# A fused Flamingo block on one Trainium2 core: probabilities transposed once per pair of batches, value products on halves of the array, one bank for key and value projections

## What is computed

```python
q = (query @ wq).reshape(bs, sq, N_Q_HEADS, D_K).transpose((0, 2, 1, 3))
k = (key @ wk) ...
v = (value @ wv) ...
q = _apply_rope(q, curr_seq_pos)
k = _apply_rope(k, curr_seq_pos)
raw = jnp.einsum('bhqd,bhkd->bhqk', q, k) / scale
masked = raw + mask[:bs, None, curr_seq_pos:curr_seq_pos + sq, :sk]
attn = jax.nn.softmax(masked, axis=-1)
out = jnp.einsum('bhqk,bhkd->bhqd', attn, v)
out = out.transpose((0, 2, 1, 3)).reshape(bs, sq, N_Q_HEADS * D_V)
return out @ wo
```

## Time and profile before

| | us |
|---|---|
| median of 3 runs | 894.86 (893.86 to 894.96) |
| span of the profiled execution | 893.8 |
| first `score` to last `outputs` matmuls of the attention stage, in that execution | about 237 to 811 |
| PE busy, share of the span | 792.5, 89% |
| DVE busy, share of the span | 723.5, 81% |

### The profile page before, as it was taken

The page is one execution under the profiler, slowest core; times in us unless marked ns, Lnnn a source line. Parts: engine busy times, 40 slices in busy tenths (PEclk is TensorE's granted clock), DMA queues, the critical chain, the costliest instruction groups (busy, mean ns, idle before and its releaser), DMA issues. The chain is left out here.

```text
span 893.8 us, 13394 instructions
## 1 busy us (share of the span) xinstructions
PE 792.5 (89%) x4276; PEld 644.9 (72%) x4276; DVE 723.5 (81%) x1282; ACT 382.5 (43%) x1095; POOL 363.9 (41%) x300
## 2 busy tenths in 40 slices
PE   2899987977899999999999989999999999984764
PEld 1555653966688888778888878888887888873653
DVE  5898987879788888768888868888885988886994
ACT  2777774322343433434343334443433443243552
POOL 2777876233542532314433313353332432203562
PEclk9999999987999999999999999999999999997896
DMA  8210120110110211101021000111100102002001
GB/s 266 77 47 23 48 76 1 36 41 7 48 48 24 60 43 29 36 14 48 24 59 48 24 26 25 48 36 47 48 25 13 48 12 54 0 1 72 12 36 47
DMA packets 37443, 37.46 MB, mean 42 GB/s; under 512 B 2896, under 2 KB 27216, under 8 KB 37392
## 3 DMA queue, kind: packets, MB, share of 16 engines
q1 hardware_dynamic: 35168, 32.81, 12.7%
q10 hardware_dynamic: 2224, 3.94, 1.4%
HBM read 34.64 MB, written 2.10 MB: 41 GB/s over the span
## 5 line engine op out<-in xcount | busy, mean ns | idle before, releaser
L917 POOL TENSOR_TENSOR dense<-rope_a,rope_b 128x512 f32<-128x512 f32 x62 | 79.4, 1280 | 236.9 <-DVE rope_b L1037 236.9
L971 ACT ACTIVATE ot_hi<-PB 128x512 fp32r<-128x512 f32 x64 | 38.3, 598 | 182.7 <-PE PB L1286 182.7
L962 ACT ACTIVATE e_sb<-masked,nmax 128x64 f32<-128x64 f32 x256 | 86.1, 337 | 70.3 <-DVE nmax L1068 70.3
L1202 PE MATMUL QB<-xT_hi,wq_lo 128*128 128x512 f32 x256 | 107.9, 421 | 1.7 <-DVE xT_lo L1113 1.7
L1202 PE MATMUL ROW<-wo_hi,ot_lo 128*128 128x512 f32 x256 | 103.5, 404 | 5.7 <-DVE ot_lo L1087 5.7
L1204 PE MATMUL QB<-xT_hi,wq_hi 128*128 128x512 f32 x256 | 101.9, 398 | 2.1 <-issue 2.1
L1203 PE MATMUL QB<-xT_lo,wq_hi 128*128 128x512 f32 x256 | 102.1, 399 | 0.0
L1203 PE MATMUL ROW<-wo_lo,ot_hi 128*128 128x512 f32 x256 | 101.9, 398 | 0.0
L1204 PE MATMUL ROW<-wo_hi,ot_hi 128*128 128x512 f32 x256 | 101.8, 398 | 0.0
L1077 DVE TENSOR_TENSOR p_dup<-e_sb,rz 128x512 f32<-128x512 f32 x64 | 98.8, 1543 | 2.2
L1037 DVE TENSOR_TENSOR rope_b<-QB,rope 64x512 f32<-64x512 f32 x124 | 85.3, 688 | 3.9
(11 more groups left out here) (200 smaller groups left out, 2014.8 us busy)
## 6 DMA issues: line engine op xcount, KB each, us to landing
raw<-in_wq SPq DMA_DIRECT2D x32, 256.0 KB, 2.8
raw<-in_wo SPq DMA_DIRECT2D x32, 256.0 KB, 2.6
ctx_two<-in_ctx SPq DMA_DIRECT2D x16, 256.0 KB, 3.8
x_sb<-in_x SPq DMA_DIRECT2D x8, 256.0 KB, 7.9
ctx_raw<-in_ctxT ACTq DMA_DIRECT2D x1, 2048.0 KB, 13.4
raw<-in_wv SPq DMA_DIRECT2D x8, 256.0 KB, 2.8
raw<-in_wk SPq DMA_DIRECT2D x8, 256.0 KB, 2.9
out<-x_sb SPq DMA_DIRECT2D x8, 256.0 KB, 2.0
```

The lines of the kernel that those rows point to most:

```text
L917: nc.gpsimd.tensor_tensor(dst, a, b, ALU.add).then_inc(s_rot, 1)
L962: nc.scalar.activation(e_sb[:, r, :], masked[:, r, :], ACT.Exp, bias=nmax[:, r:r + 1], accum_out=zsum[:, r:r + 1]).then_inc(s_exp, 1)
L1202: nc.tensor.matmul(out, lhs[1], rhs[0], start=first, stop=False)
```

## The change

**Probabilities.** They are written once (`p_sb`, 128×256, in two alternating buffers) and ordered so that two batches of the same pair of heads stand side by side; 2 transposes of 128×128 then give, in the lower 64 rows, the first batch's and in the upper 64 rows the second batch's probabilities. pt_hi and pt_lo have 256 columns instead of 512, and normalizing waits for the transposes of two slots back instead of the last.

**Value products.** `v_stk` becomes `v_hi` and `v_lo`, each 128×256 per tile, rounded and split by one instruction each instead of two of 64 rows. `weighted` is 6 matmuls of 256 columns over 64 rows: v_lo·pt_hi, v_hi·pt_lo and v_hi·pt_hi, each for the lower and for the upper half of the array's rows. The halves write to two different banks (PB2).

**Projections.** Keys and values share one bank, KV, and so a key waits until the value ahead of it has been read out, and the other way round (`kv_free`). Values move to slots 0, 2, 3 (tiles 5 to 7 of the pair) and 10, 11, 12, 14, 15 (tiles 0 to 4 of the next); none is left in the slots with a key or after slot 15, and tile 4 of the first pair is made ahead of the first slot.

```diff
+V_OWN = {0: 5, 2: 6, 3: 7}
+V_NEXT = {10: 0, 11: 1, 12: 2, 14: 3, 15: 4}
...
-        v_stk = sb("v_stk", [P, B, 2 * DH], F32R)
+        v_hi = sb("v_hi", [P, TILES, 2 * DH], F32R)
+        v_lo = sb("v_lo", [P, TILES, 2 * DH], F32R)
...
-        KB, VB, SB_, TB, PB = (bank(n) for n in ("KB", "VB2", "SB", "TB", "PB"))
+        KV, SB_, TB = (bank(n) for n in ("KV", "SB", "TB"))
+        PB2 = ctx.enter_context(nc.psum_tensor("PB", [P, 2, 512], F32))
+        PB = [PB2[:, b, 0:256] for b in range(2)]
...
-                for b in range(2):
-                    rows = slice(S * b, S * b + S)
-                    nc.scalar.activation(v_stk[rows, 2 * tile + b, :], bank[rows, 0:2 * DH], ACT.Copy)\
-                      .then_inc(s_vhi, 1)
+                nc.scalar.activation(v_hi[:, tile, :], bank[:, 0:2 * DH], ACT.Copy).then_inc(s_vhi, 1)
...
-                if n:
-                    dve.wait_ge(s_t, N)
-                nc.vector.tensor_tensor(p_dup[:, :, :, :], e_sb[:, :, :].unsqueeze(2).broadcast_to([P, 4, 2, S]),
-                                        rz[:, :].unsqueeze(2).unsqueeze(3).broadcast_to([P, 4, 2, S]),
-                                        ALU.mult).then_inc(s_p, 1)
+                if n >= 2:
+                    dve.wait_ge(s_t, N - 1)
+                nc.vector.tensor_tensor(p_sb[:, n % 2, :, :], e_sb[:, :, :],
+                                        rz[:, :].unsqueeze(2).broadcast_to([P, 4, S]), ALU.mult).then_inc(s_p, 1)
...
-                for r in range(4):
+                for r in range(2):
                     mm = nc.tensor.transpose(TB[:, r * P:(r + 1) * P],
-                                             p_dup[:, r, :, :].rearrange("p a k -> p (a k)"), ident[:, :])
+                                             p_sb[:, n % 2, 2 * r:2 * r + 2, :].rearrange("p b k -> p (b k)"),
+                                             ident[:, :])
...
-                for b in range(2):
-                    v = v_stk[:, 2 * tile + b, g * DH:g * DH + DH]
-                    cols = slice(256 * b, 256 * b + 256)
-                    nc.tensor.matmul(PB[:, cols], v, pt_lo[:, cols], start=True, stop=False)
-                    mm = nc.tensor.matmul(PB[:, cols], v, pt_hi[:, cols], start=False, stop=True)
+                for i, (v, p) in enumerate(((v_lo, pt_hi), (v_hi, pt_lo), (v_hi, pt_hi))):
+                    for b in range(2):
+                        rows = slice(S * b, S * b + S)
+                        mm = nc.tensor.matmul(PB[b], v[rows, tile, g * DH:g * DH + DH], p[rows, :],
+                                              start=(i == 0), stop=(i == 2))
...
+            def kv_free(gp, n):
+
+                if n in (2, 10, 14):
+                    pe.wait_ge(s_parts, 3 * (q_job(gp, n - 1) + 1) + 3)
+                elif n == 9:
+                    pe.wait_ge(s_parts, 3 * (q_job(gp, 5) + 1) + 3)
+                elif n in V_OWN or n in (1, 5):
+                    pe.wait_ge(s_vlo, 8 * gp + 5 + sum(m < n for m in V_OWN))
+                else:
+                    pe.wait_ge(s_vlo, 8 * gp + 8 + sum(m < n for m in V_NEXT))
```

More of the change, by code:

```diff
@@ L834, in grouped_attention @@
         e_sb = sb("e_sb", [P, 4, S])
-        p_dup = sb("p_dup", [P, 4, 2, S])
+        p_sb = sb("p_sb", [P, 2, 4, S])
         nmax = sb("nmax2", [P, 4])
@@ L838, in grouped_attention @@
         rz = sb("rz2", [P, 4])
-        pt_hi = sb("pt_hi", [P, 512], F32R)
-        pt_lo = sb("pt_lo", [P, 512], F32R)
+        pt_hi = sb("pt_hi", [P, 256], F32R)
+        pt_lo = sb("pt_lo", [P, 256], F32R)
         ot_hi = sb("ot_hi", [P, GH, P], F32R)
@@ L859, in grouped_attention @@
         TX = [SB_, TB, QB[1], OB, SB_, TB, OB, SB_]
-        FIRST_V = [VB, PB, VB, PB]
+        FIRST_V = [PB2[:, t % 2, :] for t in range(5)]
         parts = (rope_a[:, :], rope_b[:, :])
-        spare_parts = (k_rot[:, 512:1024], p_dup[:, :, :, :].rearrange("p r a k -> p (r a k)"))
+        spare_parts = (k_rot[:, 512:1024], p_sb[:, :, :, :].rearrange("p n r k -> p (n r k)"))
         views = weight_views(d)
@@ L966, in round_pt @@
                 act.wait_ge(s_t, N + 1)
-                nc.scalar.activation(pt_hi[:, :], TB[:, :], ACT.Copy).then_inc(s_pthi, 1)
+                nc.scalar.activation(pt_hi[:, :], TB[:, 0:256], ACT.Copy).then_inc(s_pthi, 1)
             def round_ot(N):
@@ L986, in round_x @@
                                      ACT.Copy).then_inc(s_xhi, 1)
-            for tile in range(4):
+            for tile in range(5):
                 round_v(0, tile, FIRST_V[tile])
@@ L1002, in pair @@
                         round_ot(N - 1)
-                    if n < 4:
-                        round_v(gp, 4 + n)
-                    if 12 <= n < 15 and ahead:
-                        round_v(gp + 1, n - 12)
+                    if n in V_OWN:
+                        round_v(gp, V_OWN[n])
+                    if n in V_NEXT and ahead:
+                        round_v(gp + 1, V_NEXT[n])
                     for r, (kind, m, slot) in enumerate(OWN):
@@ L1016, in pair @@
                 round_ot(SLOTS * gp + SLOTS - 1)
-                if ahead:
-                    round_v(gp + 1, 3)
             with act.Fori(0, PAIRS - 1) as gp:
@@ L1132, in _ @@
                 normalize_x(t)
-            rest_v(0, 3, FIRST_V[3])
+            for tile in (3, 4):
+                rest_v(0, tile, FIRST_V[tile])
             for t in range(4):
@@ L1173, in pair @@
                         rope_k(q_job(gp, n) + 1, 4 * gp + K_SLOTS.index(n) + 1)
-                    if n < 4:
-                        rest_v(gp, 4 + n)
-                    if 12 <= n < 15 and ahead:
-                        rest_v(gp + 1, n - 12)
+                    if n in V_OWN:
+                        rest_v(gp, V_OWN[n])
+                    if n in V_NEXT and ahead:
+                        rest_v(gp + 1, V_NEXT[n])
                 N = SLOTS * gp + SLOTS
@@ L1181, in pair @@
                 rest_ot(N - 1)
-                if ahead:
-                    rest_v(gp + 1, 3)
                 if not ahead:
@@ L1215, in key, with value @@
                 for k in range(KC):
-                    mm = three(KB[:, :], [w[:, k, :] for w in wk], [x[:, k, cols] for x in (ctx_hi, ctx_lo)],
+                    mm = three(KV[:, :], [w[:, k, :] for w in wk], [x[:, k, cols] for x in (ctx_hi, ctx_lo)],
                                k == 0, k == KC - 1)
                 mm.then_inc(s_k, 1)
-            def value(tile, bank=VB):
+            def value(tile, bank=KV):
                 cols = slice(P * tile, P * tile + P)
@@ L1240, in _ @@
                 if tile >= 2:
-                    pe.wait_ge(s_vlo, 2 * (tile - 1))
+                    pe.wait_ge(s_vlo, tile - 1)
                 value(tile, FIRST_V[tile])
@@ L1329, in pair @@
                             pe.wait_ge(s_piece, piece_first(gp + 1, "k", 0))
-                        pe.wait_ge(s_parts, 3 * (q_job(gp, n - 4) + 1) + 3)
+                        kv_free(gp, n)
                         key(K % 2)
-                    if n < 4:
-                        pe.wait_ge(s_vlo, 2 * (8 * gp + 4 + n))
-                        value(4 + n)
-                    if 12 <= n < 15 and ahead:
-                        if n == 12:
+                    if n in V_OWN:
+                        kv_free(gp, n)
+                        value(V_OWN[n])
+                    if n in V_NEXT and ahead:
+                        if n == min(V_NEXT):
                             pe.wait_ge(s_piece, piece_first(gp + 1, "v", 1))
-                        pe.wait_ge(s_vlo, 2 * (8 * gp + n - 4))
-                        value(n - 12)
+                        kv_free(gp, n)
+                        value(V_NEXT[n])
                 N = SLOTS * gp + SLOTS
@@ L1343, in pair @@
                 weighted(gp, N - 1, 15)
-                if ahead:
-                    pe.wait_ge(s_vlo, 2 * (8 * gp + 11))
-                    value(3)
                 outputs(gp, N - 1, 15)
```

30 lines of the change are left out of this document (14 added, 16 removed).

## The result

The kernel after the change takes 889.41 us (median; 886.02 to 891.80), against 894.53 (890.73 to 898.41) for the kernel before on the same chip: ratio 0.9943, 95% interval 0.9931 to 0.9955. So it is faster by 5.1 us, where 12.3 were forecast. The time lies inside the range of 866 to 899; the forecast's own range of 877 to 889 is just missed.

A forecast was written before the change was run, and what follows sets the result against it. PE was taken to set the pace in the attention stage. Savings of 21.7 us less 9.4 for the value products gave −12.3 on the profiled 893.8, 881.5, plus 1.1 for the median: 882.6 us, range 866 to 899.

The forecast's parts named there:

- small savings missing: Rival: savings from probability waits and from covers by moved values don't come; 889.9 us; chance 0.08.
- Transposes: Attention slots: two fewer transposes on PE, −0.22 us a slot in 56 slots, −12.3 us.
- Value products: Attention slots: six half-row products take 0.67 us a visit, +0.18 us a slot in 52 slots, +9.4 us.
- rival of loads one after another: Rival: the two halves' weights load in sequence, so a visit takes 0.96 us; 897.6 us, slower; chance 0.12.
- Waits for probabilities: Sixteen attention slots: PE's wait for DVE's probabilities goes, 0.20 us each, −3.2 us.
- Slot 11: Looped pairs: a moved value tile covers the wait for a rotated query, 0.60 us in each of three, −1.8 us.
- Pair ends: Value tile before slot 15's transposes free; outputs of 14 gain 0.27 us each, −0.8 us; removing the later value costs nothing.
- Last pair and last slots: Last pair has one value fewer, −1.5 us; its DVE-paced last slots lose 0.27 us each, −1.4 us with the tail.
- The shared bank: Keys and values waiting for each other's bank: costed at nothing.

The follow-up runs named there:

- b_head0: The kernel before with only TensorE's loop head moved to slot 0 of a 256-instruction block: 891.45 us, ratio 0.9952 to before.
- a_head0: The kernel after with only TensorE's loop head moved to slot 0 of a 256-instruction block: 877.71 us, ratio 0.9802 to before.

## Why the prediction was off

**The step that failed is one that wasn't there.** The prediction moved a value tile ahead of the loop and costed what it computes, not that its instructions shift the loop's head: it put the jump back of TensorE's loop at nothing, without a reason. The row was in view: the earlier trace rows shows the load of the first score of the second pair after an idle of 1.39 us "issue" (wait for nothing that the profile shows), and I used it for the loads' length only. The two jumps cost 4.8 us before and 11.3 after by the traces. With the head at slot 0 in both, the change is worth 891.45 − 877.71 = 13.7 us, 12.3 by the prediction. That 13.7 is so near to 12.3 is partly luck: the two medians are from two chips (13.4 by their ratios to before), the products were mis-sized by 4.6 us the other way, and the traces put only 8.8 down to the changed work behind the first score, as worked out below. None of the rivals had the jumps; the "small savings missing" rival gives 889.9, half a microsecond from the median, for a reason that isn't so: those savings came.

Step by step, from the starts of matmuls in the second pair of b_head0 and a_head0:

- **Transposes:** 0.36 us from the first to what follows, now 0.14: −0.22 a slot. As forecast.
- **Value products, mis-sized:** +0.27 a visit, not +0.18, in all 14.0 instead of 9.4: a visit takes 0.76 us, not 0.67. A visit on column halves cost 0.30 to enter and leave, on row halves 0.40. The pair's own 0.12 was right, and so was that the halves overlap. The rival of loads one after another is out too: the two loads of a pair of products last as long together as one does (PEld in after):

```profile
442.04 0.19 PEld L1282 LDWEIGHTS PB<-pt_hi,v_lo 64*128 64x128 f32 x2 [0.37 <-issue]
```

- **Waits for probabilities:** gone. They were in slots 5, 7, 9 and 11 and cost 0.24 there in the looped pairs and 0.14 to 0.17 in the last, about 3.5 us for 16, forecast 3.2.
- **Slot 11:** it has 1.44 us more of value and is 0.60 longer; with the visit, the transposes and the wait for p, the covered wait for GpSimd is 0.65, forecast 0.60.
- **Pair ends:** from slot 15's score to the next pair's 17.73 before, 17.37 after. From the last product to the outputs 1.70 us with nothing in it, where 1.69 stood before with a value tile: taking it away cost nothing, as forecast. I didn't see that this made an idle place worth filling.
- **Last pair and last slots:** the last pair, from its first score to its last, is 2.5 us shorter. The cycle of its last slots is 5.04 instead of 5.25, −0.21 for the forecast −0.27; the probabilities there take 0.42 (DVE, slot 13):

```profile
787.32 0.42 DVE L1075 TENSOR_TENSOR p_sb<-e_sb,rz 128x256 f32<-128x256 f32 x1
```

- **The shared bank:** no wait of PE for KV stands in the trace. As forecast.

Over what follows the first score, these make 3 × 1.63 for the looped pairs, 2.5 for the last and 1.3 behind it, with what rounding leaves 8.8 us. The other 5.6 of the 14.4 by which the two spans differ are before the first score (3.2, less 0.7 in slot 0) and in two pair ends of b_head0 of 19.3 us instead of 17.73, where the clock fell. In kernels with after's code up to there, the first score starts anywhere from 231.9 to 238.0 us, on average of nine at 235.2, and on average of the five of before's kind at 237.2. So some 2 us of the 3.2 can belong to the change, but single profiled executions don't settle it, nor how much of the 13.7 comes from the clock.

## What to carry to other kernels

Where an engine's loop has a body near the size of the code it can hold, compare instruction packets and the time around each jump before and after any edit ahead of or in the loop, and fix the head's place; an edit of value 14 us showed as 5 here because the head had moved. Entering and leaving a part of the array is paid once a visit, so halves pay only for visits of many products: six halves cost what six full products did. By the same numbers twelve would take 0.40 + 6 × 0.12 = 1.12 us, where twelve full ones would take about 1.44, an estimate. And if an edit takes the cover away from a wait without cost, the wait is a free place for other work.

## What the runs showed of the hardware that I had not expected

- A loop pass of 6.56 blocks of code is kept from one pass to the next with the head at slot 0 (18 packets, 5.12 us for slot 0) and fetched anew, 9 packets a pass, from slot 128 or 236, or at 7.31 blocks from slot 0.
- Where the loop isn't held, PE stands about 1 us at the jump, and again where the head's block is used up before the next has come, some 3.0 to 3.4 us later; these second stops were 1.02, 2.00 and 2.90 us. Behind 2.00 and 2.90, and behind 1.66 and 2.62 at the second jump, the granted clock fell to 0.5; behind 1.02 and 1.08 it didn't.
- Products on the two row halves start together, 10 ns apart, even when two other products of the first half stand between them in the code.
- Entering and leaving row halves costs 0.40 us a visit, a further pair of 256 columns 0.12.
